# Expert numbers in groups of eight words, loaded into eight TensorE registers at once

## What is computed

```
x = x + attention0(layernorm(x), ctx)                         # output projection and bias
x = x + ffn0(layernorm(x))     # sigmoid router, 4 of 16 experts, shared expert, residual
x = x + attention1(layernorm(x), ctx, mask)
x = x + ffn1(layernorm(x))     # softmax router, 2 of 16 experts, shared expert

ffn:  y[n] = sum over the chosen e of cw[n, e] * (silu(x[n] Wg[e]) * (x[n] Wu[e])) Wd[e]
```

## Time and profile before

| what | value |
|---|---|
| median of three runs | 3399.73 us |
| span of the profiled execution | 3384.7 us |
| TensorE busy | 2691.7 us (80%) |
| VectorE busy | 1776.4 us (52%) |
| ScalarE busy | 1492.8 us (44%) |
| GpSimd busy | 1015.5 us (30%) |
| mean granted TensorE clock | 0.929 |
| chain that ended last | PE 49%, DVE 16%, issue 14%, ACT 11%, POOL 6%, DMA 3% |

### The profile page before, as it was taken

One profiled execution on the slowest core, in us unless ns is written; L12 is line 12 of the kernel. 1 busy time (PEld: TensorE's weight loads), 2 busy tenths in 40 slices (PEclk: granted clock), 3 DMA queues, 4 the chain that ended last, 5 costly groups with the idle time before them and its releaser, 6 DMA issues.

```text
span 3384.7 us, 53365 instructions
## 1 busy us (share of the span) xinstructions
PE 2691.7 (80%) x15200; PEld 2037.1 (60%) x15201; DVE 1776.4 (52%) x5704; ACT 1492.8 (44%) x3972; POOL 1015.5 (30%) x1126
## 2 busy tenths in 40 slices
PE   7999999999994777777768999999999994777500
PEld 5666666666673666666655666666666763666400
DVE  4666667667664333333335666666666663333333
ACT  4655556555552222222225566566565561222100
POOL 2343343333333300000004434434434334000276
PEclk9999999999997998999989999999999997999755
DMA  4111111111113333333334222222222134333355
GB/s 158 54 56 48 57 54 48 59 49 51 56 51 71 127 115 102 111 110 107 114 99 143 70 68 74 69 66 76 68 63 79 63 64 94 107 116 105 115 178 172
DMA packets 202629, 294.70 MB, mean 87 GB/s; under 512 B 29910, under 2 KB 151002, under 8 KB 202076
## 3 DMA queue, kind: packets, MB, share of 16 engines
q1 hardware_dynamic: 159756, 185.09, 17.0%
q0 software_dynamic: 38224, 104.91, 10.2%
q10 hardware_dynamic: 4608, 4.20, 0.8%
HBM read 157.75 MB, written 136.34 MB: 87 GB/s over the span
## 4 chain that ended last, share of the span: by engine, by line
PE 49%; DVE 16%; issue 14%; ACT 11%; POOL 6%; DMA 3%; SPq 0%; DVEq 0%; POOLq 0%; ACTq 0%
PE ps L1309 12%; ACT W L649 9%; PE ps L1317 6%; PE ps L1143 6%; PE ps L1160 5%; PE ps L1301 4%; DVE mx L811 3%; POOL xsort L486 3%; PE ps L1185 3%; PE ps L1124 2%; PE ps L1174 2%; POOL ygath L519 2%; PE ps L1242 2%; PE ps L1322 1%; PE ps L1128 1%
## 5 line engine op out<-in xcount | busy, mean ns | idle before, releaser
L649 ACT ACTIVATE W<-ps,nmx 128x120 f32<-128x120 f32 x2048 | 539.4, 402 | 200.8 <-DVE nmx L814 200.6
L1160 PE MATMUL ps<-KB,Q 128*128 128x480 f32 x1024 | 456.9, 579 | 52.7 <-ACT W L649 48.4
L1309 PE MATMUL ps<-wgu,ygath 128*128 x1664 | 475.8, 412 | 4.5 <-issue 4.5
L1052 DVE TENSOR_TENSOR ygath<-ygath,ps 128x128 f32<-128x128 f32 x416 | 119.5, 287 | 684.2 <-ACT ygath L712 684.2
L486 POOL DMA_INDIRECT xsort<-xn,xidx x384 | 375.3, 977 | 243.8 <-DVE xidx L1002 133.5
L519 POOL DMA_INDIRECT ygath<-ysort,yidx x400 | 388.7, 972 | 154.8 <-issue 94.0
L1301 PE MATMUL ps<-cst,ygath 128*128 128x128 f32 x832 | 178.0, 298 | 276.3 <-issue 214.1
L707 ACT ACTIVATE ygath<-ps 128x256 f32<-128x256 f32 x416 | 159.4, 383 | 539.2 <-PE ps L1301 539.0
L811 DVE TENSOR_REDUCE mx<-ps 128x8 f32<-128x960 f32 x256 | 295.6, 1155 | 177.2 <-PE ps L1160 176.3
L528 POOL TENSOR_TENSOR rstd<-ve,cst 128x2 f32<-128x2 f32 x128 | 91.0, 711 | 911.4 <-DVE ve L769 909.2
L1160 PEld LDWEIGHTS ps<-KB,Q 128*128 128x128 f32 x1024 | 181.6, 189 | 261.0 <-issue 129.2
(11 more groups left out here) (153 smaller groups left out, 4211.3 us busy)
## 6 DMA issues: line engine op xcount, KB each, us to landing
ygath<-xsort SPq DMA_DIRECT2D x416, 128.0 KB, 2.0
ysort<-ygath SPq DMA_DIRECT2D x208, 256.0 KB, 2.3
based<-XO SPq DMA_DIRECT2D x64, 256.0 KB, 2.0
XL<-in_x SPq DMA_DIRECT2D x32, 256.0 KB
wgu<-in_wgu SPq DMA_DIRECT2D x2, 4096.0 KB, 14.4
XL<-based SPq DMA_DIRECT2D x32, 256.0 KB
X<-based SPq DMA_DIRECT2D x32, 256.0 KB
out_x<-X SPq DMA_DIRECT2D x32, 256.0 KB, 2.3
```

The lines of the kernel that those rows point to most:

```text
L649: ins = e.activation(prob[s][i][:, t, j, :], ps[:, sbank(s, i) + t, j * LK:(j + 1) * LK], ACT.Exp, bias=nmx[s][:, i, t, j:j + 1], scale=SCALE)
L1160: mm = e.matmul(ps[:, sbank(s, i) + t, 0:G * LK], Q[s][:, i, t * P:(t + 1) * P], KB[s][:, i, :, :].rearrange("p j k -> p (j k)"), start=Tr ...
L1309: mm = e.matmul(ps[:, 2 + h, 0:2 * F], xtT[h][:, c, :], wgu[:, bass.ds(x * (DC * 2 * F) + c * 2 * F, 2 * F)], start=(c == 0), stop=(c == D ...
```

## The change

`tab` becomes two tiles. `row_tab` holds the tiles' first rows. `exp_tab` holds, for each group of four steps, eight words side by side: first the expert numbers of tiles n-1 to n+2, then those of n-3 to n. The numbers are written there by four DMAs in place of one: for each half of the groups one DMA with 68 (second stage: 36) pieces of four words, and one for the first group, whose missing tiles stay zero. TensorE reads a group's eight words with one register load. In the built program `exp_tab` begins at byte 213408 of the partition, a multiple of 32, so each group of eight words starts at a multiple of 32 bytes. `tab` began at byte 211840, also a multiple of 32; the loads of before start at word 387+n and 389+n of it, with n a multiple of four, so never at a multiple of 16 bytes. SyncE's load starts at word n, and so always at one.

```diff
-        tab = sb("tab", [1, 2, NTMAX + 3], I32)
+        row_tab = sb("row_tab", [1, NTMAX + 4], I32)
+        exp_tab = sb("exp_tab", [1, (NTMAX // 4 + 1) * 8], I32)
...
-                for k in range(2):
-                    e.dma_start(tab[:, k, 3 * k:3 * k + NTMAX], tabd[L][k:k + 1, :]).then_inc(tb_ld, 16)
-                e.wait_ge(tb_ld, 32 * (L + 1))
+                fours = exp_tab[:].rearrange("o (w c) -> o w c", c=8)
+                n = NT[L]
+                e.dma_start(row_tab[:, 0:NTMAX], tabd[L][0:1, :]).then_inc(tb_ld, 16)
+                for c, ago in ((0, 1), (4, 3)):
+                    e.dma_start(fours[:, 1:n // 4 + 1, c:c + 4],
+                                tabd[L][1:2, 4 - ago:4 - ago + n].rearrange("o (w r) -> o w r", r=4)
+                                ).then_inc(tb_ld, 16)
+                    e.dma_start(fours[:, 0, c + ago:c + 4], tabd[L][1:2, 0:4 - ago]).then_inc(tb_ld, 16)
+                e.wait_ge(tb_ld, 80 * (L + 1))
...
-                    e.load(row_regs, tab[0:1, 0, bass.ds(n, 4)])
+                    e.load(row_regs, row_tab[0:1, bass.ds(n, 4)])
...
-            expert_regs = [[[e.alloc_register(f"expert{k}{x}{r}") for r in range(4)] for x in range(2)]
-                           for k in range(2)]
+            expert_regs = [[e.alloc_register(f"expert{k}{r}") for r in range(8)] for k in range(2)]
...
-                def experts(n, regs):
-
-                    e.load(regs, tab[0:1, 1, bass.ds(n, 4)])
-                    return [e.snap(x, min_val=0, max_val=E - 1) for x in regs]
-
                 def tile_experts_of(n, k):
 
-
-                    return experts(n + 2, expert_regs[k][0]), experts(n, expert_regs[k][1])
+                    e.load(expert_regs[k], exp_tab[0:1, bass.ds(n * 2, 8)])
+                    x = [e.snap(x, min_val=0, max_val=E - 1) for x in expert_regs[k]]
+                    return x[0:4], x[4:8]
```

More of the change, by code:

```diff
@@ L740, in _ @@
             e.memset(cnt[:], 0.0)
-            e.memset(tab[:], 0)
+            e.memset(exp_tab[:], 0)
             e.wait_ge(init, 3)
```

## The result

The changed kernel takes 3149.99 us (median of four runs, 3146.34 to 3152.11), against 3399.44 us for the kernel before. The ratio is 0.927, with a 95% interval of 0.9248 to 0.9293. The forecast was 3157 us. The profiled execution has a span of 3150.3 us, and its time is 3152.11 us, so 1.8 us lie around the span.

A forecast was written before the change was run, and what follows sets the result against it. TensorE's sequencer, held by register loads, was taken to bound the expert stages. Savings of 240 us in the loop and 6.5 outside, less 4 for tables, took the span from 3384.7 to 3142; 15 more gave 3157 us, range 3105 to 3240.

The forecast's parts named there:

- The price of the load, X: TensorE's register load of eight aligned words: 0.60 us, as two accesses at SyncE's median; bounds 0.30 and 2.9 us.
- The gaps: TensorE's idle times at the loop's top and at the prefetch: 0.69 and 0.22 us, after 0.79 and 0.81 of queued work.
- The iteration: One expert loop pass of eight tiles: 14.28 us in place of 19.09, saving 4.81 us in each of fifty.
- the refill: Expert loop: 0.37 us an iteration for TensorE's pipeline filling again behind two gaps.
- The unbroken run: TensorE between gaps in the expert stage: seven tiles in a row at 1.625 us without waiting for another engine.
- The half clock: Expert stages: slow work from a granted clock of 0.92, 1.53 us an iteration, taken as gone after the change.
- The tables: SyncE's three more table DMAs ahead of the barrier: 4 us lost in both stages together, bounds 1 and 25.
- Span and median: Whole kernel: 242.5 us off the span of 3384.7 gives 3142; the runs' median, 15 us above the span, gives 3157.
- The price by the word, aligned or not: Rival on TensorE's load: eight words cost 1.99 us whatever the alignment, 18.3 us an iteration, 3363 us; chance 0.11.
- The price by the load: Rival on TensorE's load: eight words cost what four cost, 1.0 us, 15.6 us an iteration, 3225 us; chance 0.09.
- Another engine as the bound: Rival in the expert stages: another engine limits a tile to 1.9 us in place of 1.625, 3271 us; chance 0.05.
- The load dearer than the pair: Rival at both loop points: the eight-word load takes 2.9 us, 20.8 us an iteration, 3490 us, slower; chance 0.04.

The follow-up runs named there:

- the two aligned loads: Changed kernel, but TensorE reads a group's eight words with two loads of four, each at a multiple of 16 bytes: 3187.99 us, ratio 0.9391.
- the kernel without a gap: Changed kernel, but each group's load is issued after the second step of the group before it, across the branch too: 3105.94 us, ratio 0.915.
- the series of word counts: Changed kernel, but each load brings twelve, twenty or twenty-eight words, of which eight are used: 3176.47, 3255.43 and 3341.90 us.
- the repeat: Kernel before, run once more unchanged for a second profile: 3403.01 us, span 3401.1; the changed kernel, also run again unchanged: 3146.46 us, span 3144.6.
- the unaligned kernel: Changed kernel with its table and loads moved by one word, so the eight-word load never starts at an aligned place: 3363.12 us, ratio 0.9912.

## Why the prediction was right

- *What bounds the expert stages.* Right: TensorE's sequencer with its register loads. The median moved by 249 us, and "issue" alone by 180.
- *The price of the load, X.* Forecast 0.60 us, measured 0.591. The reading behind it, that alignment and not the engine made TensorE's loads three times as long as SyncE's, was shown by the two aligned loads (0.332 us). I split 0.60 as two accesses of 0.30; it is 0.07 + 2 x 0.257. For two pieces the splits give nearly the same, which is luck: for seven they would be 2.10 and 1.87 us, and 1.872 is the shortest measured.
- *The gaps.* Forecast 0.69 and 0.22 us, 0.91 in sum. The chain shows 0.67 and 0.14. I had added 0.15 us at each place for eight registers to treat; the operations behind the load still take 0.150 in the median. At the top 0.9 us stand beside the load all the same, as in my sum (0.88), with one more register operation there (L1301) and somewhat longer steps between; at the prefetch, which has no such operation, it is 0.36 where I had 0.43.
- *The iteration.* Forecast 14.28 us, measured 14.27. This is closer than its terms: idle is 24.7 / 31 = 0.80 us, 0.1 less than forecast, and the refill 0.47 in place of 0.37. The two errors cancel, which is luck. The refill was also misread: 0.44 us of it stay in the kernel without a gap.
- *The unbroken run.* I counted seven tiles in a row at 1.625 us. Between two gaps there are six, and the chain shows five of them at that pace (1318.44 to 1326.57) and the one behind the gap slower. What I drew from it holds: no other engine got in the way.
- *The half clock.* I took it as gone, and it is. This was the least supported term, argued from one stage where TensorE is 92% busy; the series of word counts bears it out. It is worth about 1.5 of the 4.8 us.
- *The tables.* Forecast 4 us lost. The second stage lost 1.7 us. In the first 4.0 us passed from SyncE's first table DMA to its first row load, and now 3.8: there the barrier's wait for GpSimd hides the rest.
- *Span and median.* I took 242.5 us off the span of the first profile and put 15 us on again, which is the same as taking them off the median. Only 1.8 us lie around a span. The rest of the 15 was a quick execution (3384.7, with the runs at 3392 to 3406): in the repeat, 16.4 us longer, the first expert stage ends 3.0 us later (1759.6 against 1756.6), the stretch between the stages takes 9.2 more and what follows 4.2 more. By the median the saving is 249 us, 7 more than my sum. I read an iteration of 19.09 us from that quick execution, and the 7 us by which the repeat is longer outside the attention stage would account for it; a saving read from single profiles is no sharper than this, 234.4 us for the first pair (3384.7 - 3150.3) and 256.5 for the repeated one (3401.1 - 3144.6).
- *The rivals.* The price by the word, aligned or not (1.99 us), was excluded: it holds only off the boundary, where eight words do cost 1.93 us at the least. That the unaligned kernel takes 3363 us, just what I gave that rival, is luck: its loads have a median of 2.31 us and not 1.99. The 1.6 us that the prediction estimates for eight registers beside this rival are excluded for an aligned load by the same 0.591 us. The price by the load (1.0 us) was excluded by 0.332 against 0.591. Another engine as the bound: in the changed kernel's first stage every wait that the profile lists for TensorE is "issue", and with the load ahead TensorE is at 100% without a wait. The load dearer than the pair: excluded by 0.591 us; even the unaligned load, at 2.31, stays below the pair's 2.33.

## What to carry to other kernels

Read the sequencer's own rows when a busy engine shows gaps that the view calls "issue", and compare the same operation on other engines: the shortest durations told 0.30 from 1.00 us. Start tables that an engine loads into registers at a multiple of 16 bytes, and duplicate words rather than load off it; most of the gain here came from that (210 of the 249 us), not from having one load fewer (38). Then move the load to a place where more work is queued for the engine than it takes, across the loop's branch too, and reckon with more than the gap itself: here gaps that summed to 4.19 us an iteration, the longest 2.7, brought 1.5 us of lost clock with them, and gaps that summed to 1.50 none.

## What the runs showed that I had not expected

- A register load off a 16-byte boundary reads every word singly, also those in whole aligned pieces: 1.93 us at the least for eight words moved by one and by two words alike.
- Some loads take 0.3 to 0.4 us more than the shortest. In the kernel before it was one of each pair in nearly every group of the loop (1.337 beside 0.996 us); with eight aligned words in place it hits none inside the stages, with four aligned words some (up to 0.657 us), with 28 words most (2.226 in the median against 1.872). In the kernel before the long loads fall where the DMA engines are busy. These rows cover the two loads of rows 7, the long one and the short one (the last figure but one is the DMA share):

```profile
1307.20:1308.50 1.30, 0.39 (x3) 0.04 (x1) 0.84 (x3) 0.16 (x1) 0.00 (x0) 1.00 0.64 211
1308.90:1309.90 1.00, 0.00 (x0) 0.00 (x0) 0.00 (x0) 0.00 (x0) 0.00 (x0) 1.00 0.03 8
```

Over all 212 loads of that trace, 307 DMA packets in the mean are on their way during a load of over 1.25 us and 65 during a shorter one. That isn't the whole of it: the changed kernel's load at 1302.0 takes 0.598 us with a DMA share of 0.60. No run was made to tell.
- The second attention stage of one and the same kernel takes 9 us more or less with its share of half clock (a granted clock of 0.97 or 0.96), which bounds what a single profile of this kernel can tell.
